# Masked context attentions: the mask of a score tile is added by VectorE together with its maximum, not by a product on TensorE

## The reference

```python
# layer 1, context attention (layer 3 is the same without biases, its mask the other way round)
scores = jnp.einsum('bhqd,bhkd->bhqk', qh, kh) / jnp.sqrt(jnp.float32(D_K))
scores = jnp.where(mask[:, None] == 0, jnp.float32(-1000000000.0), scores)
attn = jax.nn.softmax(scores, axis=-1)
ctx = jnp.einsum('bhqk,bhkd->bhqd', attn, vh)
```

## Time and profile before

| | |
|---|---|
| median of three runs | 3376.77 us |
| the profiled execution | 3375.58 us, of which the span is 3373.6 us |
| L1x, scores and maxima | 1149.2 to 1294 us of the span |
| L3x, scores and maxima | 2915.9 to 3052 us of the span |
| PE busy in the whole span | 2740.5 us (81%) |
| DVE busy in the whole span | 2080.8 us (62%) |

### The profile page before, as it was taken

How to read it: one execution, slowest core, us unless ns; L and a number is a source line. 1 busy time by engine, 2 the same in 40 slices (tenths; PEclk the granted TensorE clock), 3 DMA queues, 4 the chain that set the end, 5 groups by cost and what they waited for, 6 DMA issues and landing times. The chain is left out here.

```text
span 3373.6 us, 44323 instructions
## 1 busy us (share of the span) xinstructions
PE 2740.5 (81%) x16400; PEld 1278.7 (38%) x16400; DVE 2080.8 (62%) x4159; ACT 1304.8 (39%) x2241; POOL 913.2 (27%) x1160
## 2 busy tenths in 40 slices
PE   4997869855566598999997999987864799698998
PEld 1332424411121254345554444443432233354555
DVE  5884761287788654566676556556677777463444
ACT  1664543243334254222121434333632466364221
POOL 2101100074475310233341545552135110110000
PEclk9997879977887798999999999997976899798999
DMA  5121300000000220111231000002100320320000
GB/s 130 35 39 44 61 27 1 37 14 0 0 0 0 53 51 4 27 30 37 66 73 44 1 1 1 1 1 50 27 1 3 55 44 16 97 40 1 1 1 13
DMA packets 45494, 95.04 MB, mean 28 GB/s; under 512 B 14168, under 2 KB 33420, under 8 KB 39520
## 3 DMA queue, kind: packets, MB, share of 16 engines
q1 hardware_dynamic: 45280, 92.22, 12.4%
HBM read 46.20 MB, written 1.38 MB: 14 GB/s over the span
## 5 line engine op out<-in xcount | busy, mean ns | idle before, releaser
L1638 POOL TENSOR_TENSOR mamba_dbu<-mamba_du,mamba_b 128x512 f32<-128x512 f32 x128 | 257.0, 2041 | 131.3 <-ACT mamba_b L1621 131.3
L1605 PE MATMUL ps<-mamba_hc,weights 128*128 128x512 f32 x256 | 163.6, 729 | 98.4 <-DVE mamba_hc L1663 97.8
L1652 DVE TENSOR_TENSOR_SCAN mamba_h<-mamba_da,mamba_dbu 128x512 f32<-128x512 f32 x128 | 210.9, 1650 | 18.3 <-ACT mamba_da L1626 18.3
L542 DVE TENSOR_REDUCE L3a_negmax<-ps 128x1 f32<-128x512 f32 x256 | 162.4, 684 | 52.1 <-PE ps L302 51.6
L542 DVE TENSOR_REDUCE L0a_negmax<-ps 128x1 f32<-128x512 f32 x256 | 162.6, 685 | 50.6 <-PE ps L302 50.1
L2438 DVE TENSOR_REDUCE skv_negmax<-ps 128x2 f32<-128x1024 f32 (+3 forms) x128 | 101.2, 799 | 129.4 <-PE ps L2281 129.4
L405 ACT ACTIVATE L0a_probs<-ps 128x512 f32<-128x512 f32 x256 | 143.7, 599 | 77.3 <-PE ps L321 75.6
L405 ACT ACTIVATE L3a_probs<-ps 128x512 f32<-128x512 f32 x256 | 143.7, 599 | 73.4 <-PE ps L321 71.9
L2500 ACT ACTIVATE skv_probs<-ps 128x1024 f32<-128x1024 f32 (+3 forms) x128 | 90.2, 705 | 186.9 <-PE ps L2307 186.9
L164 POOL TENSOR_SCALAR vareps<-mv 128x4 f32<-128x4 f32 x24 | 7.6, 315 | 549.4 <-DVE mv L1279 495.1
L189 PE MATMUL ps<-stream,xT 128*64 128x512 f32 x512 | 129.4, 623 | 14.4 <-DVE moa_v L2063 7.2
(11 more groups left out here) (619 smaller groups left out, 6586.3 us busy)
## 6 DMA issues: line engine op xcount, KB each, us to landing
moa_masks<-picked SPq DMA_DIRECT2D x32, 512.0 KB, 6.5
stream<-stream SPq DMA_DIRECT2D x32, 192.0 KB
stream<-gate_up_down_in SPq DMA_DIRECT2D x1, 4352.0 KB, 13.0
stream<-value_output_in SPq DMA_DIRECT2D x1, 4096.0 KB, 12.0
moa_gateb<-gates SPq DMA_DIRECT2D x32, 128.0 KB
stream<-ffn_in SPq DMA_DIRECT2D x1, 2888.0 KB, 9.4
L0a_qs<-L0a_qs SPq DMA_DIRECT2D x16, 128.0 KB
L0x_qs<-L0x_qs SPq DMA_DIRECT2D x16, 128.0 KB
```

The lines of the kernel that those rows point to most:

```text
L542: dve.tensor_reduce(negmax[:, hh // G % 4, a, hh % G:hh % G + 1], ps[:, i % S_RING, :], AX.X, ALU.max, negate=True).then_inc(s["maxed"], 1)
L1605: pe.matmul(ps[:, 4 + j, :], k.ident, hc[:, (J * n + j) % RING, :], start=n == 0, stop=n == N - 1).then_inc(s["summed"], 1)
L1638: pool.tensor_tensor(dbu[:, i % RING, :], du[:, j, :], bsb[:, n % AHEAD, :], ALU.mult).then_inc(s["dbu_ready"], 1)
L1652: dve.tensor_tensor_scan(out=hs[:, i % RING, :], data0=da[:, i % RING, :], data1=dbu[:, i % RING, :], initial=0.0, op0=ALU.mult, op1=ALU.a ...
```

## The change

PE no longer makes the mask product, and no longer waits for `mask_q`. DVE takes each half of a tile by itself with one operation that adds the mask to the scores, negates the sum and keeps the minimum of a row. That operation also writes the negated sums, 128 x 154 in bf16, to a new buffer `masked` that nothing reads. So a tile has two DVE instructions in place of one. The wait for `mask_q` stands on DVE, which makes `mask_q` itself. L0x and L2x are unchanged, and so is `mask_k`.

```diff
+            masked = sb("masked", [P, 2, 2, CTX], BF16)
...
-                        if masks and h == 0:
-                            pe.wait_ge(s["mask_q"], b + 1)
...
-                                         ks[:, b % 2, h, :], start=p == 0, stop=not masks, skip_group_check=True)
-                    if masks:
-                        both = ps[:, i % S_RING, :].rearrange("p (t k) -> p t k", t=2)[:, :, 0:CTX]
-                        last = pe.matmul(both, wb(k, "ident"), mask_q[:, b % 2, 2 * u:2 * u + 2, :], start=False, stop=True,
-                                         skip_group_check=True)
+                                         ks[:, b % 2, h, :], start=p == 0, stop=True, skip_group_check=True)
...
+                    if masks:
+                        if hh % H == 0 and u == 0:
+                            dve.wait_ge(s["mask_q"], hh // H + 1)
+                        for p in range(2):
+                            at = ps[:, i % S_RING, 256 * p:256 * p + CTX]
+                            last = dve.tensor_tensor_reduce(masked[:, i % 2, p, :], at, mask_q[:, hh // H % 2, 2 * u + p, :], -1.0, 3e38, ALU.add,
+                                                            ALU.min, negmax[:, hh // G % 4, 2 * u + p, hh % G:hh % G + 1])
+                        last.then_inc(s["maxed"], 1)
+                        return
```

## The result

The changed kernel takes 3346.2 us, the median of six runs (3342.5 to 3355.1). The kernel before has 3370.9 us in the six runs that stand beside them (3366.8 to 3377.4; the first three of these gave the 3376.8 from which the forecast was counted). The ratio is 0.9927, with an interval of 0.991 to 0.9943, which is 24.6 us less. The direction was right and the size was not.

A forecast was written before the change was run, and what follows sets the result against it. PE was taken to set the pace in the masked stages, with DVE having slack. The terms -28.0 + 5.2 + 1.2 + 2.3 + 1.8 + 1.5 gave -16.0 us, from 3376.8 to about 3361 us, range 3349 to 3404.

The forecast's parts named there:

- PE's slots: Masked stages L1x and L3x: removing the mask product frees 0.13 us of PE for each of 108 tiles, -28.0 us.
- c: DVE's time for a queued tile with the new operation: 0.61 us, bounds 0.46 and 0.76.
- rival 1: DVE's second output costs nothing, a queued tile takes 0.46 us: -21 us, 3356; chance 15%.
- (a): Layer norm, twice in each masked stage: PE waits longer for `x_tok`, 1.3 us each, +5.2 us.
- (b): Quads 1, 9 and 17, with values and `mask_k` on DVE: 0.2 us each, +1.2 us in all.
- (c): Stage starts: first turned score comes 2.0 us later in L3x and 0.3 in L1x, +2.3 us.
- (d): Start of L3x: without the mask product PE's clock stays at half speed longer, +1.8 us.
- The clock behind waits: PE's waits at the layer norm can also lower its clock: +1.5 us allowed for both masked stages.
- L2x and its like: Stage L2x, which makes no mask product: forecast unchanged.
- Rival 3: DVE becomes the bound at two cycles a column, 0.93 us a tile: +27 us, 3403; chance 13%.

The follow-up runs named there:

- both: Changed kernel with PE's mask product kept beside DVE's new operation, so the mask is added twice; ratio 1.0005 to the kernel before.
- chained: Changed kernel with the second half of each tile waiting for the first by a semaphore on DVE; ratio 0.9942 to the kernel before.
- no_mask: Changed kernel with DVE's plain reduction of unmasked scores and no PE mask product; turned scores still masked; ratio 0.9923 to the kernel before.
- best: Changed kernel with the output bias four quads later, plain reduction, and no `mask_q` or its transfer; 3330.6 us, ratio 0.9886 to the kernel before.
- start_product: Changed kernel with PE's mask product and DVE's single reduction kept for the first 20 tiles of both stages; ratio 0.9938 to the kernel before.
- plus_one: Changed kernel with one more DVE half operation for each tile, into a buffer nothing reads; ratio 0.9974 to the kernel before.
- bias_late: Changed kernel with POOL adding the output bias (`add_bias`) four quads later; ratio 0.9912 to the kernel before.

## Why the prediction was right in direction and wrong in size

- **PE's slots, -28.0.** Right: 1.05 us for each pair of quads against 1.04, and `both` shows that without it there is no gain. That L811 counts for 0.13 us and not for its mean of 0.313 was the step that mattered most: by the mean the product would have been worth 68 us.
- **c, 0.61 us.** Wrong, and the main mis-sized term: by the forecast's own sums for 0.61 and 0.46 it is 5 of the 8.6 us that were missed. The step that failed is "I take one queued small instruction, 0.077": the rows show no time for the accumulator read in a queue, and rival 1's 0.46 was the value (0.47 measured). The operation itself, 0.24 queued and 0.315 alone, was right to 0.01. `chained` sets c to 0.60 and gives back 2.7 us in L3x. In L1x it has 148.7 us, between the two records of the change.
- **(a) The waits for `x_tok`, +5.2.** Too large, and the second mis-sized term: about 1.2 in all. In L3x the interval of quad 14 holds a wait of 0.35 us (4.17 against 3.82) and that of quad 22 none (3.81), where I had 1.3 each. Even at c = 0.60 it is 0.9 and 0.3, so the step also failed in taking quad 22 to be like quad 14. Why the first is 0.9 and not 1.3 I did not follow. In L1x the pause is 3.28 us, 0.9 more than before (forecast 1.2 more), and quad 22 has none.
- **(b) Quads 1, 9 and 17, +1.2.** Nothing: the intervals of these quads fell by 0.52 and 0.53 us, as those of their neighbours did.
- **(c) The start, +2.3.** In L3x +0.3 in place of +2.0. At c = 0.60 it is +2.0, so that step was right for its c. In L1x -1.3 in place of +0.3, but that is no effect of the change that I could settle: `both`, with all products, has 14.2 us, and `no_mask`, with none, 14.4. In the records of before and of `no_mask` PE waited 1.72 and 1.73 us for the transfer of `L1x_ks` ahead of late scores, in the change 0.56 and in `both` no such wait stands out; and ahead of the first T it waits for another transfer in all four. `best`, which has one transfer fewer, takes 12.0.
- **(d) The clock at the start of L3x, +1.8.** Right: 1.7 by `start_product`, of the 2.0 us that the stage loses. What I missed is that L1x loses the same, 1.6 us; the comparison with before hides it, because L1x of before had a late clock of its own.
- **The clock behind waits, +1.5.** It exists, in L1x alone, but behind a pause that was there before. Take from the intervals of quads 14 and 15 those of quads 16 and 17 and the pause: 1.9 us are left in before (8.62 - 4.34 - 2.40) and in `both`, 1.7 and 4.8 in the two records of the change: a spread, not a term.
- **L2x and its like.** Unchanged, as forecast (119.1 against 120.0).

Rival 3's two cycles a column did not come: 154 columns took 0.24 us of the queue. Rival 1 had c right and said -21, because it kept (a) near 3 us, (b) at 1 and the clock at 3. With the measured terms L3x sums to -14.0 + 0.4 (start) + 1.8 (clock between T and W: 1.0 longer, and 0.8 of removed product lie in it) + 0.3 (wait) = -11.5, which the stage has. In L1x the steady part gives 12.4 us in one record and 9.3 in the other, and the start 2.7 and 3.0 against the one record of before, of which `both` shows up to 3.2 to be scatter. That late clock in the record of before, and the 6.3 us outside the stages, make the profiles differ by more than the medians, -24.6 (-30.3 to -19.2); the record of before lies 4.7 us above its median and that of the change 3.8 below.

The absolute time missed by more than the terms did. The three runs from which I counted had a median of 3376.8, the six 3370.9, and 3370.9 - 16 would have been 3355. At its low end the range had 4 us to spare below rival 1 with the clock's loss left out, which is less than this scatter of 6, and the measured time fell 2.8 us below it.

## What to carry to other kernels

Here a step that took work from the bound engine to one with slack gained what the work held of the queue, from start to start, and cost nothing in the ordinary quads, where the receiving engine met its ring's deadlines (c up to 0.60 us); at the starts, where it did not, it cost. So write the loss as a function of the one unknown (here c): the sum held from 0.60 to 0.95 us to within 4 us, when the chosen value did not. Where the new operation has a result for each row beside its main one, look whether a reduction already in the trace has it for free before charging an instruction for it. Look at a pause that was there before as well: the freed time made it longer here, and moving the one instruction that blocked a queue took 3.7 us out of that quad. Then look at every stage that shares the code: in L2x the same edit made two other waits longer.

## What the runs showed of the hardware

- An accumulator read of 83 ns starts together with the next operation of DVE; the queue moves on by 0.24 us for 154 columns, which by estimate is 0.16 at the forecast's slope of 1.01 ns a column and 0.08 fixed. The row's own 315 ns is not what it costs in a queue.
- A semaphore between two such short operations is not free: the second half starts 0.36 us behind the first in place of 0.24. The Trainium skill (VectorE: DVE Perf Modes, section The DRAIN you can't avoid) says that a semaphore after each of eight copies cost nothing extra; at this length the runs differ from it by 0.12 us each.
- After a pause of PE of 2.4 to 3.4 us in quad 14 of L1x the clock falls to one half (1.2 GHz) for a time that differs from record to record: in the windows shown the shortfall is (1 - 0.79) x 8 / 0.5 = 3.4 us of half clock in one record of the changed kernel and 5.0 + 5.3 in the other. It moves the stage by 3 us and is no difference between kernels; `chained` and `start_product` had the 3.4 us too, `no_mask` and `plus_one` some 10. Behind the pause of 1.06 us in `bias_late` the clock stayed at 1.00.
